# Attention row maxima shipped in pairs, three small moves in the expert stage: a pre-norm attention + mixture-of-experts layer on one core

## What is computed

```python
# attention: 16 heads of 64, one shared key and value head
xn  = layernorm(layernorm(x)) ; q = xn @ Wq ; k, v = split(xn @ Wkv)
sim = einsum('bhid,bjd->bhij', q, k) * 64**-0.5
out = einsum('bhij,bjd->bhid', softmax(sim), v) ; x = x + layernorm(out @ Wo)
# experts: 8 of them, each token goes to the 2 likeliest
probs = softmax(h @ gate_w.T) ; topw, sel = top_k(probs, 2) ; topw /= sum(topw)
gate, up = split(h @ gate_up_w[e]) ; y_e = (up * gelu(gate)) @ down_w[e]
x = x + sum over the two chosen experts of topw * y_e
```

## Time and profile before

| | |
|---|---|
| three timed runs | 604.35, 604.46 and 606.38 us; median 604.46 us |
| the profiled execution | 608.39 us in all, its span 606.6 us, 1.8 us around it |
| TensorE | 571.6 us busy, 94% of the span |
| VectorE | 398.2 us, 66% |
| ScalarE | 296.9 us, 49% |
| GpSimd | 395.7 us, 65% |
| granted TensorE clock | 0.984 of full speed in the mean |

### The profile page before, as it was taken

How to read it: one execution, slowest core, us unless ns; L and a number is a source line. 1 busy time by engine, 2 the same in 40 slices (tenths; PEclk the granted TensorE clock), 3 DMA queues, 4 the chain that set the end, 5 groups by cost and what they waited for, 6 DMA issues and landing times. The chain is left out here.

```text
span 606.6 us, 8802 instructions
## 1 busy us (share of the span) xinstructions
PE 571.6 (94%) x2543; PEld 325.6 (54%) x2543; DVE 398.2 (66%) x873; ACT 296.9 (49%) x559; POOL 395.7 (65%) x329
## 2 busy tenths in 40 slices
PE   8799999999999999998999999899997878999992
PEld 6464455444545454444545445344433567788881
DVE  4878656657756869774676878875584468444453
ACT  3235655445636564553655455355536553444550
POOL 5438776667758866799696579849747934445333
PEclk9889999999999999999999999899999999999997
DMA  5111011010201200071000000000005300231033
GB/s 166 71 72 71 2 71 71 5 72 1 75 1 72 74 2 1 7 243 69 1 5 0 2 7 21 13 2 4 11 0 151 94 23 27 58 81 52 23 126 98
DMA packets 27518, 29.46 MB, mean 49 GB/s; under 512 B 7732, under 2 KB 18742, under 8 KB 27473
## 3 DMA queue, kind: packets, MB, share of 16 engines
q1 hardware_dynamic: 24912, 24.27, 12.6%
q0 software_dynamic: 2272, 4.24, 2.1%
q10 hardware_dynamic: 288, 0.39, 0.2%
HBM read 13.50 MB, written 15.32 MB: 48 GB/s over the span
## 5 line engine op out<-in xcount | busy, mean ns | idle before, releaser
L1195 ACT ACTIVATE prob<-s_ps 128x512 f32<-128x512 f32 x256 | 150.8, 599 | 183.3 <-PE s_ps L1292 180.7
L1115 DVE TENSOR_REDUCE less_max<-max_ps 128x1 fp32r<-128x512 f32 x256 | 174.0, 689 | 82.5 <-PE max_ps L1270 79.7
L1041 POOL TENSOR_TENSOR fold<-prob 128x1024 f32<-128x1024 f32 x63 | 149.9, 2380 | 88.3 <-ACT prob L1195 87.6
L1306 PE MATMUL pv_ps<-prob,v 128*64 128x512 f32 x512 | 138.5, 621 | 0.0
L1290 PE MATMUL s_ps<-q_hl,khh 128*128 128x512 f32 x256 | 117.9, 461 | 0.7 <-ACT prob L1195 0.7
L1270 PE MATMUL max_ps<-khh,q_hl 128*128 128x512 f32 x256 | 103.0, 408 | 5.3 <-DVE less_max L1115 4.7
L1292 PE MATMUL s_ps<-q_hm,kly 65*128 65x512 f32 x256 | 101.8, 398 | 0.0
L1290 PEld LDWEIGHTS s_ps<-q_hl,khh 128*128 128x128 f32 x256 | 48.6, 190 | 86.2 <-ACT prob L1195 67.0
L1047 POOL TENSOR_TENSOR psums<-fold 128x512 f32<-128x512 f32 x63 | 80.9, 1285 | 4.9
L1270 PEld LDWEIGHTS max_ps<-khh,q_hl 128*128 128x128 f32 x256 | 49.1, 192 | 23.4 <-DVE less_max L1115 11.0
L1292 PEld LDWEIGHTS s_ps<-q_hm,kly 65*128 65x128 f32 x256 | 48.8, 191 | 9.2 <-issue 3.4
(11 more groups left out here) (251 smaller groups left out, 769.8 us busy)
## 6 DMA issues: line engine op xcount, KB each, us to landing
sorted_rows<-raw_w SPq DMA_DIRECT2D x36, 260.0 KB, 2.6
raw_w<-in_gate_upT SPq DMA_DIRECT2D x8, 512.0 KB, 9.2
wd<-in_downT SPq DMA_DIRECT2D x8, 256.0 KB
raw_w<-parts SPq DMA_DIRECT2D x7, 256.0 KB, 3.2
psums<-sorted_rows SPq DMA_DIRECT2D x22, 65.0 KB, 1.7
x<-in_x SPq DMA_DIRECT2D x4, 256.0 KB, 4.4
xs_first<-sorted_rows SPq DMA_DIRECT2D x15, 65.0 KB, 1.8
out<-x SPq DMA_DIRECT2D x3, 256.0 KB, 2.3
```

The lines of the kernel that those rows point to most:

```text
L1041: nc.gpsimd.tensor_tensor(fold[:, :, :], prob[:, head % 4, 0:2, :], prob[:, head % 4, 2:4, :], ALU.add).then_inc(prob_folded, 1)
L1115: nc.vector.tensor_reduce(less_max[:, group % 2, col:col + 1], max_ps[:, k % 2, :], AX_X, ALU.max, negate=True).then_inc(max_done, 1)
L1195: nc.scalar.activation(prob[:, head % 4, jt, :], s_ps[:, k % 2, :], ACT.Exp, scale=SCALE).then_inc(exp_done, 1)
L1306: last = nc.tensor.matmul(pv_ps[DH * hd:DH * hd + DH, :], v[:, b % 2, jt, :], prob[:, head % 4, jt, :], start=(jt == 0), stop=(jt == JT - 1))
```

## The change

Five edits, in the order of the program:

1. **Maxima in pairs.** `shifts` ships heads 0 to 15 two at a time and later ones four at a time; `less_max` gets three buffers instead of two. There are 20 SHIFTs instead of 17.
2. **The order of the first 64 EXP steps.** Ten maxima instead of twelve stand ahead of slot 0, and then one comes every 0.78 slots until the usual lead of 22 is reached; two of the unread products go with the two maxima. The first SHIFT stands ahead of the QLO of pair 1, and the Q steps of pairs 2 and 3 move from slots -3 and 3 to 0 and 4.
3. **List spans made early.** What `list_rest` computed from data of the first three batches is now computed when the second list is finished, in the attention block.
4. **Additions sooner.** `add_parts` of the first three batches moves to turns 36, 37 and 38.
5. **Last loads in halves.** Both loads of the last batch become two of 128 KB, and the first half has a semaphore of its own.

```diff
-        place(-8 if pair == 1 else at + 1, 4, "QLO", u, p)
+        place(-7.4 if pair == 1 else at + 1, 4, "QLO", u, p)
...
-        place(n - 15 if n < 12 else (n - 12) // 2 if n < 32 else n - 16 - lead, 1, "MAX", u, a)
+        place(n - 15 if n < 10 else 0.78 * (n - 10) if n < 64 else n - 16 - lead, 1, "MAX", u, a)
...
-FIRST_Q_AT = (-3, 3)
-
-FIRST_SHIFT_AT = (-7.5, 2)
+FIRST_Q_AT = (0, 4)
+
+FIRST_SHIFT_AT = (-7.5, 4.5)
...
+MAX_SLOTS = 3
...
-    return [(0, 2), (2, 2)] + [(head, 4) for head in range(4, units * UH, 4)]
+    return [(head, 2) for head in range(0, 16, 2)] + [(head, 4) for head in range(16, units * UH, 4)]
...
             if kind == "LIST3":
                 set_list(dve, first, count)
+                if n == len(LIST_TILES) - 1:
+                    link(dve, nc.vector.tensor_reduce(starts[:, E:2 * E], steps_old[:, :, :], AX_X, ALU.add))
+                    link(dve, nc.vector.tensor_copy(starts[:, 0:E], begun[:, 0:E]))
+                    link(dve, nc.vector.memset(starts[:, 2 * E:2 * E + 1], 0.0))
+                    link(dve, nc.vector.tensor_tensor(jumps[:, 0:E], starts[:, 1:E + 1], starts[:, 0:E], ALU.subtract))
...
+                    link(dve, nc.vector.tensor_tensor(lengths[:, 0:E], starts[:, E:2 * E], starts[:, 0:E], ALU.subtract))
+                    part_ends(dve, 0)
+
+        def part_ends(dve, n):
+
+            part = slice(n * E, (n + 1) * E)
+            other = lengths[:, part].unsqueeze(1).broadcast_to([P, E, E])
+            link(dve, nc.vector.tensor_tensor(cmp[:, n, :, :], other, tri[:, :, :], ALU.mult))
+            link(dve, nc.vector.tensor_reduce(ends[:, part], cmp[:, n, :, :], AX_X, ALU.add))
+            link(dve, nc.vector.tensor_tensor(ends[:, part], ends[:, part], lengths[:, part], ALU.add))
...
-                        if 2 <= k < 12:
+                        if 2 <= k < 10:
                             keep_busy(BUSY["rows"])
...
+            def load_last(eng, n):
+
+                for half in range(2):
+                    t = slice(half * TPB // 2, (half + 1) * TPB // 2)
+                    eng.dma_start(part_in[:, LB, n, t, :], parts[n * T + LB * S:n * T + NB * S, :].rearrange(
+                        "(p t) d -> p t d", t=TPB)[:, t, :]).then_inc(half_in if half == 0 else parts_in[LB], 16)
...
-                    if NT - 2 <= k < NT - 2 + LB:
-                        add_parts(k - (NT - 2), slice(0, TPB))
+                    if NT - 3 <= k < NT - 3 + LB:
+                        add_parts(k - (NT - 3), slice(0, TPB))
```

More of the change, by code:

```diff
@@ L699, in list_rest @@
                 link(dve, nc.vector.tensor_reduce(more[:, :], steps_more[:, :, :], AX_X, ALU.add))
[L700 to L703, removed]
                 link(dve, nc.vector.tensor_tensor(lengths[:, E:2 * E], more[:, :], starts[:, E:2 * E], ALU.subtract))
[L705 to L709, removed]
+                part_ends(dve, 1)
                 link(dve, nc.vector.tensor_tensor(ends[:, E:2 * E], ends[:, E:2 * E],
@@ L955, in _ @@
                             slot = (head + h) % Q_SLOTS
-                            first = (head % 4 + h) * JT
+                            first = h * JT
                             sp.dma_start(q_hm[DH:DH + 1, slot:slot + 2, :].bitcast(F32),
@@ L1105, in _ @@
                         head, it = divmod(k, JT)
-                        group, i = divmod(head, 4)
+                        n = max(n for n, (first, _) in enumerate(shift_heads) if first <= head)
                         dve.wait_ge(max_mm, k + 1)
-                        col = i * JT + it
-                        if i == 0 and it == 0 and group >= 2:
-                            dve.wait_ge(mrow_ready, group)
-                        if head == 2 and it == 0:
-                            dve.wait_ge(mrow_ready, 1)
-                        nc.vector.tensor_reduce(less_max[:, group % 2, col:col + 1], max_ps[:, k % 2, :], AX_X,
+                        col = k - shift_heads[n][0] * JT
+                        if col == 0 and n >= MAX_SLOTS:
+                            dve.wait_ge(mrow_ready, n - MAX_SLOTS + 1)
+                        nc.vector.tensor_reduce(less_max[:, n % MAX_SLOTS, col:col + 1], max_ps[:, k % 2, :], AX_X,
                                                 ALU.max, negate=True).then_inc(max_done, 1)
@@ L1118, in _ @@
                         head, heads = shift_heads[u]
-                        group = head // 4
                         dve.wait_ge(max_done, (head + heads) * JT)
@@ L1465, in _ @@
                     sent(sp, k)
-                load_part(sp, LB, 0)
+                load_last(sp, 0)
                 store_half(sp, 0)
@@ L1551, in _ @@
                         after_vector(dve, kind, LB, bank)
-                    if NT - 2 <= k < NT - 2 + LB:
-                        add_parts(k - (NT - 2), slice(0, TPB))
+                    if NT - 3 <= k < NT - 3 + LB:
+                        add_parts(k - (NT - 3), slice(0, TPB))
                 for half in range(2):
-                    add_parts(LB, slice(half * TPB // 2, (half + 1) * TPB // 2))
+                    add_parts(LB, slice(half * TPB // 2, (half + 1) * TPB // 2), half_in if half == 0 else parts_in[LB])
             @block2.scalar
```

14 lines of the change are left out of this document (8 added, 6 removed).

## The result

| | median of the timed runs | ratio to the kernel before |
|---|---|---|
| before | 604.46 us (603.58 to 606.38) | 1 |
| changed | 610.57 us (609.67 to 611.52) | 1.0084, 95% interval 1.0064 to 1.0103 |

By the ratio the change costs 5.1 us, by the two medians 6.1, and the interval of the ratio holds both. It was forecast to gain 1.25 us, and the range ended at 605.9 us. The profiled execution of the changed kernel took 609.67 us (span 607.8), only 1.3 us more than that of before (608.39, span 606.6), which lay 3.9 us over its kernel's median.

A forecast was written before the change was run, and what follows sets the result against it. It took TensorE as saturated from 45 us, so only its early losses, its waits for VectorE and the kernel's end could move time. -0.3 + 1.0 - 0.95 - 0.35 - 0.65 = -1.25 us, from 604.46 to 603.2 us, range 600.0 to 605.9.

The forecast's parts named there:

- The start, up to V: First steps of attention: V would start at 37.35 us instead of 39.27.
- the wait for QLO: Ahead of V: VectorE's QLO queues behind ScalarE's QHI, itself behind two exponentials; QLO of pair 2 begins near 29.7 us.
- The start, behind V: TensorE from V on: full clock, with 1.2 GHz only from 24.5 to 27.9 us; the start gains 0.3 us.
- Rival 3: Slower: TensorE, idle more often with one maximum per score, stays at 1.2 GHz; 606.0 us, chance 0.12.
- The seven maxima: Maxima owed after V, where TensorE is full: 7 x 0.235 = 1.65 us lost.
- Three more SHIFTs and denser transfers at nothing: Between 45 and 110 us: 2.5 us more VectorE work and blanking transfers twice as dense, both costed at nothing.
- Rival 4: Blanking transfers go ahead of rows, two rows late by 2.6 us: 608.4 us; chance 0.04 together with the rest.
- The end of attention, +1.0: Nine list operations ahead of the last two additions delay the sum that ends the block: 1.0 us lost, bounds 0 and 1.97.
- Turns 10 and 11, -0.95: Expert loop: operations removed from these turns let VectorE go on sooner; 0.95 us gained, bounds 0 and 1.57.
- The send, -0.35: Kernel's end: the send at 594.07 us, 1.34 us long beside VectorE's additions, takes 0.97; 0.35 us gained.
- The halves, -0.65: Last loads: the first half is added while the second is on its way; 0.65 us gained, bounds nothing and 0.8.
- I take the difference over: Whole kernel: the profiled execution lay 3.9 us above the timed median, and the forecast carries that difference over.

The follow-up runs named there:

- experiment 2: Changed kernel with the first steps ordered as in the kernel before, maxima still leaving in pairs: 605.54 us, 0.9989 of the kernel before.
- Experiment 4: Changed kernel plus unread products at TensorE's three waits ahead of V: 17 more gave 608.21 us, 1.0050 of the kernel before; 27 more gave 607.34 us, 1.0011.

## Why the prediction was wrong, step by step

**The start, up to V: right.** Forecast were 22.15 us from the first maximum to V (37.35 - 15.20), measured 21.98, and the wait for QLO was the one named. The first score came at 24.01 instead of 25.0. It was not luck: each step of the chain, reckoned from the first maximum, came within 0.4 us of its forecast (V stands at 36.56 and not at 37 to 38 us because the first maximum came 0.6 us sooner). What was off is the other end. The profile of before has V later than most: with the old order V comes 22.5 to 24.1 us behind the first maximum, in the middle of eleven profiles (all but the one with its waits filled) 23.3. Against that the gain up to V is 1.3 us and not 2.1.

**The start, behind V: this is the step that failed.** The step is the clock taken for the stretch from V on: it read "With 1.2 GHz from 24.5 to 27.9 us as now, and full clock after". TensorE was at 1.2 GHz again from 37.1 to 44.0 us, where V, PV and scores filled it, and that cost 3.45 us. Rival 3 had this mechanism with one spell of 3.4 us and 1.7 us of loss, and 0.12 of the chance, "Against: from slot 6 on PV fills TensorE". Its sign, a clock of 0.50 beyond 40 us, is what the trace shows. A full engine after V did not keep the clock up: the low clock came behind the waits ahead of V and ran on into the full stretch. Experiment 4 shows the cause, since products that nobody reads, put into those waits, took both spells away.

**The seven maxima: mis-sized.** They were priced as work alone, 1.65 us. They also bring waits, 2.4 us here and 2.4 to 2.7 in the other kernels with this rule, of which the starts of seven maxima account for 2.05: maxima that used to be made while TensorE had nothing else now stand in the full stretch, some two in a row, paced by VectorE's 0.69 us reductions. The term of the start, forecast as 0.3 us gained, is 7.47 - 2.09 = 5.4 us lost in the trace: 3.45 of clock, 1.65 of maxima and 2.4 of waits, less 2.09.

**Three more SHIFTs and denser transfers at nothing: right** (experiment 2). Rival 4 is out: the six waits of TensorE that the trace shows between 45 and 110 us were all ended by VectorE, none by a transfer, with 85 GB/s beside it:

```profile
60.00:110.00 50.00, 49.50 (x205) 24.52 (x202) 35.88 (x68) 26.17 (x49) 33.33 (x21) 1.00 0.23 85
```

**The end of attention, +1.0: right.** 1.12 us in the trace, and 0.0018, 1.1 us, between two kernels of one group, whose intervals overlap.

**Turns 10 and 11, -0.95: right**, 1.07 measured. **The send, -0.35: right**, 0.37. **The halves, -0.65: right in kind**, 0.85 measured. The prediction set against it a loss of 1.2 us, worked out from the fixed cost in the Trainium skill's page DMA: Bandwidth & Descriptors, Anatomy of one DMA. The page gives that cost for transfers that GpSimd issues, and does not say that a second transfer pays it after the first. Here, issued by SP and ScalarE 0.4 us apart, the second halves landed 0.6 us behind the first ones, so most of the 2.3 us that a first half took from issue to landing ran side by side with the second's.

**"I take the difference over".** The median was got by taking 3.9 us off the profiled execution. Of these, that execution had lost 1.7 us to a spell at 389.8 us, behind its wait at 388 us, and 0.9 in the turns, and its V was late besides. The changed kernel's profile had none of this. So the two spans differ by 1.2 us where the medians differ by 6.1. By stages the change costs 7.47 behind V and 0.14 up to step 216, less 2.09 up to V, and 1.12 at the end of attention, less 1.07, 0.37 and 0.85: 4.35 us. With V's middle place in the old order (1.3 gained instead of 2.1) it is 5.2 us, an estimate from several profiles, and the timed ratio says 5.1.

## What to carry to other kernels

Moving work around an engine's early idle time is not free when low-clock spells come behind its waits, as here behind waits of 1.4 to 2.4 us: count where the waits stand, and price the stretch behind each at the lower clock too, above all where that stretch is full. Work put off from a stretch with slack to a full one costs its own time and its dependences. Small operations cost nothing only ahead of a wait of their own engine, so look for that wait first; moving nine of them from one side of two additions to the other was worth 1.1 us in the traces. And a profile is one execution: before its span is compared with another's, list the low-clock spells in each, and see how much a stretch that no edit touched differs.

## What was not expected of the hardware

In eighteen profiles of these kernels (with before and changed) every spell at 1.2 GHz between 45 and 480 us began within 2 us of the end of one of three waits of TensorE. Behind the wait of 1.6 to 1.7 us at 275 us one followed in 5 of 16, behind that of 1.5 to 1.6 us at 388 us in 1 of 15, behind that of 1.4 to 2.3 us ahead of the last sum in 5 of 9, and there, where the wait was 0.4 us or less or was filled, in none of 9. But the five with a spell at the last sum are the same five that have one at 275 us. Of the nine without that wait, seven keep the wait at 275 us, and none of the seven has a spell there either. So the spells at the two places go together, and this count does not show that moving the nine operations is what kept the clock up at the sum. For example, of the kernel with all edits behind the start (the timeline, then windows):

```profile
273.85 0.47 PE L1213 MATMUL q_ps<-xh,wkh 128*128 128x512 f32 x1 [1.60 <-POOL xl L1059]
```

```profile
274.00:275.00 1.00, 1.00 (x5) 0.82 (x6) 0.00 (x0) 0.18 (x1) 0.98 (x2) 1.00 0.02 8
275.00:276.00 1.00, 1.00 (x5) 0.34 (x5) 0.33 (x1) 0.91 (x2) 1.00 (x1) 0.59 0.21 67
276.00:277.00 1.00, 1.00 (x4) 0.00 (x0) 0.95 (x2) 0.00 (x0) 1.00 (x1) 0.50 0.00 0
```

TensorE is busy in all three microseconds; what stands ahead of the spell is the wait, and only in some executions does a spell follow. What decides in which stays open. It also stays open why the kernel with the wait ahead of the sum filled was slow: its profile had no spell from 34 us to the end of TensorE's work, but that execution (605.00 us, clock 0.992) was the fastest of the twelve, and the other eleven had 0.981 to 0.988.

Small VectorE operations of 0.17 us sometimes took over 2 us, always while GpSimd ran a `fold` of 2.4 us, here in the changed kernel:

```profile
450.58 2.36 POOL L1051 TENSOR_TENSOR fold<-prob 128x1024 f32<-128x1024 f32 x1 [3.10 <-ACT prob L1201]
...
450.61 0.22 DVE L675 TENSOR_REDUCE tile_j<-passed 128x8 f32<-128x64 f32 x1
450.86 2.11 DVE L676 TENSOR_TENSOR tile_j<-places,tile_j 128x8 f32<-128x8 f32 x1
```

The Trainium skill's page SBUF — State Buffer, Who interferes with whom, has a rule for it: a VectorE instruction with two inputs in SBUF contends with a GpSimd instruction that reads SBUF, and one with a single input, as a reduction, does not. The trace agrees: the operation with two inputs ended at 452.97 us, 0.03 behind the `fold`, and the reduction with one input, at 450.61, kept its 0.22 us beside the same `fold`.
